# First block's attention in two halves, the weights' low parts subtracted on GpSimd, and a new order of steps

## The reference

```python
x = x + ln(attn_block(ln(x)));  x = x + ln(moe(ln(x)))
# attn_block(x), 16 heads of 16 features
h = ln(x) * w + b
xc = silu(causal_conv4(h));  q, k = l2norm(h @ Wq), l2norm(h @ Wk);  v = ln(h @ Wv)       # per head
u = sigmoid(xc @ Wig + big) * k * v;  gamma = sigmoid(xc @ Wg + bg)
mem[t] = gamma[t] * mem[t-1] + u[t]
out = group_norm(ln(mem) * q) * sigmoid(xc @ Wog + bog)
h = x + out @ Wo;  h2 = ln(h)
return h + (silu(h2 @ Wgate) * (h2 @ Wval)) @ Wout                                          # 1024 wide
# moe(x): a shared expert 704 wide with a gate of its own, and the best 2 of 8 experts, 176 wide
```

## Time and profile before

| | |
|---|---|
| median of three runs | 600.58 us |
| the profiled execution, its span | 603.1 us |
| PE busy | 518.9 us (86%) |
| DVE busy | 394.2 us (65%) |
| ACT busy | 263.7 us (44%) |
| POOL busy | 109.5 us (18%) |
| mean granted TensorE clock | 0.933 of full |

### The profile page before, as it was taken

One profiled execution on the slowest core, in us unless ns is written; L12 is line 12 of the kernel. 1 busy time (PEld: TensorE's weight loads), 2 busy tenths in 40 slices (PEclk: granted clock), 3 DMA queues, 4 the chain that ended last, 5 costly groups with the idle time before them and its releaser, 6 DMA issues.

```text
span 603.1 us, 7985 instructions
## 1 busy us (share of the span) xinstructions
PE 518.9 (86%) x2408; PEld 407.6 (68%) x2408; DVE 394.2 (65%) x1159; ACT 263.7 (44%) x469; POOL 109.5 (18%) x133
## 2 busy tenths in 40 slices
PE   2845358999569999999999998999997899999981
PEld 1413234677446587886677786788876799999871
DVE  6786643879865798875497774434657666767236
ACT  4721444425374424276631444311344456666204
POOL 1510003200002323002204000050004034444300
PEclk9985679999959999999999999999989999999986
DMA  8950000001110002021001011010129234444364
GB/s 292 380 178 15 20 2 0 1 2 35 35 35 1 0 19 89 4 66 36 1 5 67 1 35 36 0 70 2 36 71 281 77 94 119 136 124 117 106 226 139
DMA packets 29547, 44.52 MB, mean 74 GB/s; under 512 B 3083, under 2 KB 24203, under 8 KB 29163
## 3 DMA queue, kind: packets, MB, share of 16 engines
q1 hardware_dynamic: 24515, 33.07, 17.8%
q0 software_dynamic: 3408, 9.38, 4.2%
q10 hardware_dynamic: 1584, 1.57, 0.9%
HBM read 27.67 MB, written 16.34 MB: 73 GB/s over the span
## 4 chain that ended last, share of the span: by engine, by line
PE 71%; DVE 15%; ACT 7%; DMA 4%; issue 2%; POOL 0%; ACTq 0%; POOLq 0%; SPq 0%; DVEq 0%
PE psum L786 14%; PE psum L745 12%; PE psum L746 11%; PE psum L747 11%; PE psum L812 5%; PE psum L755 4%; PE psum L833 3%; DMA RDNR<-rdn 2%; PE psum L861 2%; DVE XC L1244 2%; PE psum L829 2%; PE psum L847 2%; PE psum L986 1%; PE psum L956 1%; PE psum L939 1%
## 5 line engine op out<-in xcount | busy, mean ns | idle before, releaser
L650 ACT ACTIVATE SM<-psum 128x512 f32<-128x512 f32 (+1 forms) x56 | 33.2, 594 | 123.0 <-PE psum L747 99.7
L1369 DVE TENSOR_TENSOR SM<-SM,psum 128x512 f32<-128x512 f32 (+1 forms) x56 | 38.2, 683 | 56.4 <-ACT SM L650 56.3
L526 POOL DMA_INDIRECT x_dispatched<-XN,dest x32 | 32.5, 1017 | 159.2 <-DVE XN L1437 150.7
L786 PE MATMUL psum<-WOU,SM 128*128 128x256 f32 x256 | 60.2, 380 | 0.0
L786 PEld LDWEIGHTS psum<-WOU,SM 128*128 128x128 f32 x256 | 48.3, 190 | 10.7 <-issue 2.4
L517 POOL TENSOR_TENSOR OG<-QKV,hvec 128x256 f32<-128x256 f32 x16 | 13.4, 836 | 228.1 <-ACT IG L592 214.5
L812 PE MATMUL psum<-WQKV,HT 128*128 128x512 f32 (+1 forms) x128 | 47.5, 520 | 6.5 <-ACT QKV L585 3.1
L535 POOL DMA_INDIRECT y_routed<-GO,g_dest x39 | 37.8, 968 | 67.8 <-ACT GO L720 67.5
L786 PE MATMUL psum<-SDN,SM 128*128 128x256 f32 (+1 forms) x192 | 44.8, 382 | 0.0
L812 PEld LDWEIGHTS psum<-WQKV,HT 128*128 128x128 f32 x128 | 24.9, 201 | 28.0 <-issue 21.6
L786 PEld LDWEIGHTS psum<-SDN,SM 128*128 128x128 f32 (+1 forms) x192 | 35.9, 189 | 6.5 <-issue 1.3
(11 more groups left out here) (295 smaller groups left out, 1301.4 us busy)
## 6 DMA issues: line engine op xcount, KB each, us to landing
XG<-x_dispatched SPq DMA_DIRECT2D x39, 130.0 KB, 2.7
YF<-y_routed SPq DMA_DIRECT2D x4, 1024.0 KB, 9.0
RUPR<-rup SPq DMA_DIRECT2D x1, 2816.0 KB
X<-x SPq DMA_DIRECT2D x4, 512.0 KB, 6.8
x_after_attention<-X SPq DMA_DIRECT2D x4, 512.0 KB, 2.9
QKV<-x ACTq DMA_DIRECT2D x3, 512.0 KB, 3.5
y_shared<-SH SPq DMA_DIRECT2D x3, 512.0 KB, 2.9
SHF<-y_shared SPq DMA_DIRECT2D x1, 1536.0 KB, 18.9
```

The costliest lines, as they stand in the source:

```text
L526: nc.gpsimd.indirect_dma_start(XD[:, :], bass.IndirectOffsetOnAxis(dest[:, i, old + j:old + j + 1], 0), XN[:, j, :], None).then_inc(dispat ...
L650: nc.scalar.activation(SM[0:rows, g % 3, 0:tb], p_pair(n)[0][0:rows, 0:tb], ACT.Silu).then_inc(silu_ready, 1)
L786: last = nc.tensor.matmul(p_down[:, j // 2, (j % 2) * D:(j % 2 + 1) * D], SM[0:rows, g % 3, j * P:(j + 1) * P], weight[0:rows, m, :], star ...
L1369: nc.vector.tensor_tensor(SM[0:rows, g % 3, 0:tb], SM[0:rows, g % 3, 0:tb], value_rows(n, rows)[:, 0:tb], ALU.mult).then_inc(hid_ready, 1)
```

## The change

Five things:

- Block 0's attention from `rs` to `h2` is done in two parts of two token tiles each (`PARTS`); blocks 1 to 3 stay whole. Semaphores count parts: `PSTART[b]` is the number of parts before block b.
- Block 0 has PSUM banks of its own for each step and part (`FIRST_BANK`), a pair for each of the gates g0, g1, g2, SBUF of its own for the squares (`first_sq`) and for the bias tile (`first_qb`), and puts the squares of `mt` and `centre` into SH. The waits that guarded the shared places go for block 0.
- The subtractions of `split` (wgtL, wvlL, wrL, and later supL) go from DVE to POOL. In the list of block 0 they stand behind q 3 on POOL; ACT's rounding stands behind its sigmoids of g1.
- The first steps have a list of their own for each engine, `FIRST`; `PLACE` has new positions for blocks 1 to 3 (45 for 47 steps, since `split` 0 and 1 are out of `ATTENTION`). `_order()` is as before.
- POOL scales v ahead of the bias tile and q.

The diff, cut; lines with only "..." stand for what is left out, the tables of positions above all:

```diff
 ATTENTION = (
-    [("q", 0), ("split", 0), ("q", 1), ("split", 1)] + [("q", j) for j in range(2, J)] + [("rs", 0), ("rs", 1), ("g", 0), ("g", 1)]
+    [("q", j) for j in range(J)] + [("rs", 0), ("rs", 1), ("g", 0), ("g", 1)]
...
+PARTS = [[(0, TILES[0] // 2), (TILES[0] // 2, TILES[0])]] + [[(0, n)] for n in TILES[1:]]
+PSTART = [sum(len(PARTS[a]) for a in range(b)) for b in range(NB + 1)]
...
+FIRST = {
+    "pe": """
+        ht:0 q:0 q:1 q:2 q:3 g:0 g:1 ut:0a mt:0a g:2 ut:0b mt:0b og:0a og:0b wo:0a wo:0b ht:+0 h2:0a h2:0b""",
+    "act": """
+        ln0:2 ht:0 xs:0 q:0 q:1 q:2 q:3 g:0 g:1 split:0 split:1 mt:0a mt:0b g:2 centre:1a centre:1b fetch:+0 og:0a
+        og:0b y0:0a y0:0b ln0:+2 ln2:1a ht:+0 h2:0a ln2:1b h2:1a h2:0b h2:1b xs:+0""",
+    "dve": """
+        ln0:0 ln0:1 ln0:2 conv:0 conv:1 conv:2 conv:3 q:0 q:1 rs:0a rs:1a u:0a u:1a u:2a q:2 u:3a q:3 rs:0b rs:1b u:0b
+        scan:0a scan:1a u:1b u:2b u:3b var:0a rstd:0a scan:0b scan:1b norm:0a affine:0a affine:1a var:0b rstd:0b
+        mean:1a norm:0b affine:0b affine:1b mean:1b centre:1a centre:1b var:1a var:1b rstd:1a norm:1a rstd:1b norm:1b
+        o:0a ln0:+0 ln0:+1 wo:0a o:0b ln0:+2 ln2:0a ln2:1a wo:0b ln2:0b ln2:1b conv:+0 conv:+1 conv:+2 conv:+3 h2:1a
+        h2:1b""",
+    "pool": """
+        q:0 q:1 q:2 q:3 split:0 split:1""",
+}
...
 def steps(engine):
+    yield from first(engine)
+    attention = [(PLACE[engine][b - 1][i], s[0], b + (s in AHEAD), s[1], 0) for b in range(1, NB)
+                 for i, s in enumerate(ATTENTION) if b + (s in AHEAD) < NB]
...
+        def g_banks(b, m):
+            return psum[:, 2 * m:2 * m + 2, :] if b == 0 else p_main
+        FIRST_BANK = {"ut": 6, "mt": 0, "og": 2, "wo": 4, "h2": 6}
+        def token_rows(stage, b, part, nj):
+            if b == 0:
+                return psum[:, FIRST_BANK[stage] + part, 0:nj * D]
+            return p_main.rearrange("p a n -> p (a n)")[:, 0:nj * D]
...
# POOL, at()
+                    nc.gpsimd.tensor_tensor(vj, vj, per_dim(1, 0), ALU.mult).then_inc(v_scaled, 1)
+                    link(nc.gpsimd.tensor_tensor(heads(q_bias(b)[:, m:m + 1, :]), qj, per_dim(1, 3), ALU.mult))
                     nc.gpsimd.tensor_tensor(qj, qj, per_dim(1, 2), ALU.mult).then_inc(q_scaled, 1)
-                    nc.gpsimd.tensor_tensor(vj, vj, per_dim(1, 0), ALU.mult).then_inc(v_scaled, 1)
+                if stage == "split" and b == 0:
+                    k, _ = resident[m]
+                    pool.wait_ge(w_hi, m + 1)
+                    for c in range(C):
+                        nc.gpsimd.tensor_tensor(lo[k][:, c, :], raw[k][:, c, :], f32(hi[k][:, c, :]), ALU.subtract).then_inc(w_lo, 1)
+                    if m == 0:
+                        pool.wait_ge(wr_hi, 1)
+                        nc.gpsimd.tensor_tensor(wrL[:, :, :], wr[:, :, :], f32(wrH[:, :, :]), ALU.subtract).then_inc(wr_lo, 1)
...
# ACT, at()
-                    if n >= 2:
+                    if b > 0:
                         act.wait_ge(ss_done, n - 1)
...
# PE, at()
                 if (stage, m) == ("ht", 0):
-                    if b > 0:
-                        pe.wait_ge(hr_ready, b)
+                    if b == 1:
+                        pe.wait_ge(normed, prior)
+                    if b > 1:
+                        pe.wait_ge(hr_ready, prior)
...
                 if stage == "ut":
-                    pe.wait_ge(u_ready, b + 1)
-                    pe.wait_ge(gate_ready, C * (3 * b + 2))
-                    to_features(p_main, lambda j: QKV[:, j, 2 * D:3 * D], nj).then_inc(ut_psum, 1)
+                    pe.wait_ge(u_ready, u + 1)
+                    if b == 0:
+                        pe.wait_ge(qkv_copied, new)
+                    else:
+                        pe.wait_ge(gate_ready, C * (3 * b + 2))
+                    to_features(feature_rows("ut", b, part, len(mine)), lambda j: QKV[:, t0 + j, 2 * D:3 * D], len(mine)).then_inc(ut_psum, 1)
...
# DVE, at()
-                if stage == "split" and b == 0:
-                    k, _ = resident[m]
-                    dve.wait_ge(w_hi, m + 1)
-                    for c in range(C):
-                        nc.vector.tensor_tensor(lo[k][:, c, :], raw[k][:, c, :], f32(hi[k][:, c, :]), ALU.subtract).then_inc(w_lo, 1)
-                    if m == 0:
-                        dve.wait_ge(wr_hi, 1)
-                        nc.vector.tensor_tensor(wrL[:, :, :], wr[:, :, :], f32(wrH[:, :, :]), ALU.subtract).then_inc(wr_lo, 1)
```

More of the change, by code:

```diff
@@ L111, with first @@
     "pe": [
[10 rows of a table removed]
[6 rows of a table added]
     ],
     "act": [
[10 rows of a table removed]
[6 rows of a table added]
     ],
     "dve": [
[10 rows of a table removed]
[6 rows of a table added]
     ],
     "pool": [
[10 rows of a table removed]
-    ],
-}
[6 rows of a table added]
+    ],
+}
+FIRST = {
[13 more added lines that the diff above has]
+}
+def first(engine):
+    for name, which in (step.split(":") for step in FIRST[engine].split()):
+        part = "ab".find(which[-1])
+        yield name, int(which[0] == "+"), int(which.strip("+ab")), max(part, 0)
 def steps(engine):
-    attention = [(PLACE[engine][b + 1][i], s[0], b + (s in AHEAD), s[1]) for b in range(-1, NB)
-                 for i, s in enumerate(ATTENTION) if 0 <= b + (s in AHEAD) < NB]
+    yield from first(engine)
+    attention = [(PLACE[engine][b - 1][i], s[0], b + (s in AHEAD), s[1], 0) for b in range(1, NB)
+                 for i, s in enumerate(ATTENTION) if b + (s in AHEAD) < NB]
     for n, step in enumerate(ORDER):
@@ L270, in build, with squares, q_bias, head_squares @@
         MSQ = IG[:, :, :].rearrange("p c t -> p (c t)")
+        def squares(b, m):
+            return first_sq[:, m, :] if b == 0 else SQ[(START[b] + m) % 2]
+        def q_bias(b):
+            return first_qb if b == 0 else QB
+        def head_squares(b, t0, nj):
+            if b == 0:
+                return SH[:, t0:t0 + nj, :].rearrange("p j d -> p (j d)")
+            return MSQ[:, 0:nj * D]
+        with ExitStack() as first_names:
+            first_qb = first_names.enter_context(nc.sbuf_tensor("first_qb", [P, TILES[0], D], F32))
         XTH, XTL = sb("XTH", [P, C, TB], F32R), sb("XTL", [P, C, TB], F32R)
@@ L527, in at @@
                                                          XN[:, j, :], None).then_inc(dispatched, 16)
-            for name, b, m in steps("pool"):
-                at(name, b, m)
+            for name, b, m, part in steps("pool"):
+                at(name, b, m, part)
             for i in range(NG):
@@ L582, in at @@
                     if b > 0 and m == 0:
[L583 removed]
+                        act.wait_ge(wo_psum, prior)
                     act.wait_ge(qkv_psum, n + 1)
@@ L629, in at @@
                 if (stage, m) == ("ln2", 1):
-                    act.wait_ge(ln2_stats, b + 1)
-                    for j in range(nj):
+                    act.wait_ge(ln2_stats, u + 1)
+                    for j in mine:
                         nc.scalar.activation(HN[:, j, :], HR[:, j, :], ACT.Identity, bias=l2n[:, j:j + 1],
@@ L643, in at @@
                     for c in range(C):
-                        nc.scalar.activation(H2H[:, c, 0:tb], GA[:, c, 0:tb], ACT.Copy).then_inc(h2_hi, 1)
+                        nc.scalar.activation(H2H[:, c, cols], GA[:, c, cols], ACT.Copy).then_inc(h2_hi, 1)
                 if stage in ("mup", "hid"):
@@ L691, in at @@
                                              scale=gate[:, b % 2, j:j + 1]).then_inc(sh_ready, 1)
-            for name, b, m in steps("act"):
-                at(name, b, m)
+            for name, b, m, part in steps("act"):
+                at(name, b, m, part)
             def group(stage, i):
@@ L836, in at @@
                 if stage == "ut":
[L837 to L839 removed]
+                    pe.wait_ge(u_ready, u + 1)
+                    if b == 0:
+                        pe.wait_ge(qkv_copied, new)
+                    else:
+                        pe.wait_ge(gate_ready, C * (3 * b + 2))
+                    to_features(feature_rows("ut", b, part, len(mine)), lambda j: QKV[:, t0 + j, 2 * D:3 * D], len(mine)).then_inc(ut_psum, 1)
                 if stage == "mt":
[L842 removed]
+                    pe.wait_ge(mem_ready, C * (u + 1))
                     if b == 0:
                         pe.wait_ge(centring_ready, 1)
[L845 removed]
+                    rows = token_rows("mt", b, part, len(mine))
+                    for j in mine:
                         for c in range(C):
[L847 removed]
+                            at_row = (j - t0) * D + c * P
+                            last = nc.tensor.matmul(rows[:, at_row:at_row + P],
                                                     IG[:, c, j * P:(j + 1) * P], centring[:, :], start=True, stop=True)
@@ L856, in at @@
                         pe.wait_ge(w_in["wo"], 16)
-                    pe.wait_ge(o_ready, C * (b + 1))
-                    for j in range(nj):
```

(22 more changed lines are left out.)

233 lines of the change are left out of this document (126 added, 107 removed), and 64 rows, old and new, of the table PLACE.

## The result

The changed kernel takes 606.94 us (median of ten runs, 604.26 to 611.66); the kernel before took 602.01 beside it (ten runs, 600.44 to 603.92). The ratio is 1.008, with a 95% interval of 1.0053 to 1.0108: slower, by 4.9 us. Forecast were 604.0, of a median of 600.58: +3.4. In the profiled executions the span goes from 603.1 to 608.1.

A forecast was written before the change was run, and what follows sets the result against it. DVE, PE and ACT handing the same tokens round were taken to bound the front, PE the rest. Span 603.1 + 5.4 (to mdn 7) - 1.8 (join) = 606.7, 604 us as a median; range 588 to 609.

The forecast's parts named there:

- The deciding term: Block 0's second-half rs: VectorE steps wait for whole GpSimd subtractions, so the first u ends at 46.5 us, +9.3.
- The front: Block 0's attention up to mup 0: mup 0 starts at 99.5 us, a delay of 3.3 with q 1 counted.
- supL: Subtraction on GpSimd amid block 1's affine, mean and centring: 2 x 3.34 us, costing VectorE some 4.5.
- The join: Block 0's MLP meeting block 1's: wo ahead of x2's statistics brings ht, XN and h2 forward, -1.8 us.
- Behind it: Blocks 2 and 3: new tables could return PE's 5 us of waits or cost 1.5; taken as nothing.
- B: Front and block 1: a long GpSimd subtraction lets VectorE in or costs it some 0.6; 592 us, chance 0.28.
- C: Turns hold, but g2 at full clock, the join and blocks 2 and 3 return the loss; 599.5 us, chance 0.14.
- D: Front and block 1: GpSimd subtractions into fp32r take half as much again, 3.6 for 1024 columns; 610.5 us, chance 0.08.

The follow-up runs named there:

- e3: The changed kernel with all its moved subtractions (wgtL, wrL, wvlL and supL) back on VectorE: 598.58 us, ratio 0.993 to the kernel before.
- e1: The changed kernel with only the front's subtractions (wgtL, wrL, wvlL) back on VectorE, supL still on GpSimd: 602.26 us, ratio 0.998 to the kernel before.
- e2: The changed kernel with only supL back on VectorE, the front's subtractions still on GpSimd: 605.4 us, ratio 1.004 to the kernel before.
- e4: The changed kernel with GpSimd writing zeros (memset) in place of its subtractions, which are left out of the computation: 591.77 us, ratio 0.982 to before.
- e5: The changed kernel with each GpSimd subtraction cut into four pieces (256 columns, 352 for supL): 599.55 us, ratio 0.994 to the kernel before.
- e9: The changed kernel with each GpSimd subtraction cut into eight pieces (128 columns, 176 for supL): 594.91 us, ratio 0.986 to the kernel before.
- e11: The changed kernel with each GpSimd subtraction cut into 16 pieces (64 columns, 88 for supL): 595.54 us, ratio 0.990 to the kernel before.
- e12: e9 with GpSimd's twelve scalings of each block also cut into halves of 128 columns: 593.80 us, ratio 0.985 to the kernel before.

## Why the prediction was right

**The deciding term.** "A DVE step and a GpSimd step take turns, and each waits for the whole of the other" was read off steps of 0.73 and carried to 2.5. It held: five steps of VectorE passed beside the front's subtractions, as forecast, four at 2.3 and one, beside wrL, at 0.65. The second half's first `u` ended 8.6 us later than in e3, where the prediction's deciding term had 9.3. The front's subtractions ran from 34.79 to 44.72, 9.9 us for 10.6 forecast; the Trainium skill's figure (GPSIMD Engine Reference, section 3.1) had given an estimate of 9.9, and the trace agrees. The second half's first `u` ended at 45.8 instead of 46.5. e1 to e3 show the price at the end, e4 that neither GpSimd's being busy nor its writes cause it, e5 and e9 that it goes by the length of one instruction.

**The front.** First `rs` ends 29.4 (forecast 29.3); ut b ends at 56.0 (56.5), DVE waits 2.7 for it (2.6); g2 takes 5.72, where 5 was taken between 3.5 and 6.37; `mup` 0 starts at 98.2 (99.5), and with q 1 ahead of it the front's delay is 2.2 where 3.3 was forecast. Of the 1.1 between them 0.7 is the shorter subtractions, the rest smaller errors.

**supL.** 3.64 a piece, for 3.34. Two 1.23 us steps became 4.24 and 4.06, which is 5.8 where 4.5 was forecast; this is the term most under-sized. `mdn` 7 ends 5.9 later than before (forecast 5.4), but by another road: `mup` 4, forecast 1.7 later than before, starts at 130.2 in both kernels, so that all of the 5.9 arises behind it, where 3.7 was forecast.

**The join** returned 2.2 (forecast 1.8): `mup` 0 of block 1 starts 3.75 later than before.

**Behind it** the prediction took nothing, between a return and a cost of 1.5. From there to the end the changed kernel takes 424.3 and the one before 423.1, 1.2 more in one execution of each. The waits of PE behind 185 us, first of before, then of after, have one row that grew:

```profile
PE psum L745 <- DVE SM L1369: 3.0, 2, 2.0
```

```profile
PE psum L805 <- DVE SM L1446: 6.3, 4, 2.8
```

The same row is 4.5 in e3 and 4.9 in e9. And e1 to e5, e9 and e11 have the same instructions behind this point as the changed kernel, and need 420.9 to 424.3 there, 424.3 being its own. A difference of 1.2 lies within that spread; the rows do not show that the new tables cost anything.

**The sum and the luck in it.** The sum of the prediction was +3.6 of span; measured are +5.0. The front was forecast 1.1 too dear, the stretch from there to `mdn` 7 1.6 too cheap, the join 0.4 too dear and the rest 1.2 too cheap, so part of the agreement is errors that cancel. The direction was hardly forecast either: the chances were 0.36 for slower and 0.37 for faster, and the range of 588 to 609 took in both. What was right is the mechanism and the size of its main term.

**The rivals.** B (a long subtraction lets VectorE in) is refuted by the steps of 2.3 us; what it promised, 592, is about what e4 shows (591.77) for GpSimd instructions that read nothing, and e12 and e9 come within 2 to 3 us of that by short instructions. C, no change, is refuted as a whole: g2 took 5.72, not the 3.4 to 3.7 of the full clock, the join returned only 0.4 more than forecast, and nothing came back behind it. D (dearer into fp32r) is refuted: 2.34 us for 1024 columns, and 0.72 for 256, the same as for fp32 scalings.

## What to carry to other kernels

Beside a GpSimd instruction that reads SBUF, a VectorE step on SBUF operands waited here for its whole length, and the loss sits inside VectorE's busy time: look for small steps that suddenly have the length of a GpSimd instruction. Give GpSimd such work in short pieces (here 128 columns, 0.46 us, two of VectorE's small steps): the same change is +0.8% with instructions of 1024 and 1408 columns and -1.4% with pieces of 128 and 176. And measure a front's gain at the point from which the bounding engine stays full, not at one step that an order can pull forward.
